# Turning W2 by DMA behind tiles 4 to 11, loading W1 later, and making the blocks of W1 W2^T beside value tiles 16 to 23

## The reference

```
xn  = (x - mean) / sqrt(var + 1e-5)
Q, K, V = xn W1 + b1,  xn W2 + b2,  xn W3 + b3
attn = softmax(Q K^T / 32)
out  = x + (attn V) W4 + b4 + ffn(xn)
ffn: [xr, xi] = split(xn);  [xr Wr^T - xi Wi^T + br,  xr Wi^T + xi Wr^T + bi]
Wr, Wi (512 x 512): unfolded from small tensor-train factors
```

## Time and profile before

| | us |
|---|---|
| median of 3 runs | 1287.73 (1287.54 to 1432.36) |
| profiled execution | 1288.47 |
| its span, slowest core (6) | 1286.9 |
| spans of the 8 cores | 1284.8 to 1286.9 |
| TensorE busy | 1265.2 (98%) |
| VectorE busy | 520.5 (40%) |
| ScalarE busy | 327.0 (25%) |
| GpSimd busy | 169.9 (13%) |

### The profile page before, as it was taken

How to read it: one execution, slowest core, us unless ns; L and a number is a source line. 1 busy time by engine, 2 the same in 40 slices (tenths; PEclk the granted TensorE clock), 3 DMA queues, 4 the chain that set the end, 5 groups by cost and what they waited for, 6 DMA issues and landing times.

```text
span 1286.9 us, 16235 instructions; the slowest of 8 cores (1284.8 to 1286.9 us)
## 1 busy us (share of the span) xinstructions
PE 1265.2 (98%) x5959; PEld 585.4 (45%) x6078; DVE 520.5 (40%) x856; ACT 327.0 (25%) x467; POOL 169.9 (13%) x123
## 2 busy tenths in 40 slices
PE   6999999999999999999999999999999999999998
PEld 4554444444444444444444444444444444444443
DVE  4457460544244414442444244434444244414442
ACT  2453333321211232112222311132212212221111
POOL 2232132211011101111111111111111011101110
PEclk9999999999999999999999999999999999999999
DMA  9899671133122322231233132220332022222222
GB/s 134 196 229 224 150 143 42 33 79 79 41 66 66 66 58 74 66 66 34 77 71 82 33 66 66 66 66 35 79 78 71 34 66 66 66 65 66 66 66 66
DMA packets 187294, 102.83 MB, mean 80 GB/s; under 512 B 169272, under 2 KB 171344, under 8 KB 187216
## 3 DMA queue, kind: packets, MB, share of 16 engines
q1 hardware_dynamic: 181600, 93.37, 31.0%
q0 software_dynamic: 5408, 8.39, 4.5%
q10 hardware_dynamic: 208, 0.02, 0.0%
HBM read 51.43 MB, written 16.78 MB: 53 GB/s over the span
## 4 chain that ended last, share of the span: by engine, by line
PE 98%; DMA 1%; issue 1%; POOL 0%; ACT 0%; DVE 0%; POOLq 0%; ACTq 0%; DVEq 0%
PE ring L795 34%; PE po L837 33%; PE ring L672 9%; PE po L654 4%; PE pf L654 4%; PE pf L822 2%; PE ring L755 2%; PE pf L815 2%; PE pf L808 2%; PE po L709 1%; PE pf L709 1%; DMA V<-W 1%; PE ring L643 1%; PE po L868 1%; PE pf L868 1%
## 5 line engine op out<-in xcount | busy, mean ns | idle before, releaser
L795 PE MATMUL ring<-XT,GT 128*128 128x512 bf16 x2006 | 445.0, 379 | 2.4 <-ACT Et L616 0.2
L837 PE MATMUL po<-V,ET 128*128 128x512 bf16 x1947 | 436.2, 379 | 1.9
L795 PEld LDWEIGHTS ring<-XT,GT 128*128 128x128 bf16 x2048 | 200.3, 98 | 242.1 <-issue 0.6
L837 PEld LDWEIGHTS po<-V,ET 128*128 128x128 bf16 x1984 | 194.1, 98 | 234.1
L482 DVE TENSOR_REDUCE mx<-ring 128x1 f32<-128x512 f32 x256 | 176.7, 690 | 222.0 <-PE ring L795 222.0
L508 DVE SCALAR_TENSOR_TENSOR xr<-po,rrv,xr 128x1024 f32<-128x1024 f32 x31 | 39.8, 1284 | 419.7 <-PE po L837 419.7
L333 POOL TENSOR_TENSOR xr<-xr,cb 128x1024 f32<-128x1024 f32 x32 | 75.1, 2346 | 941.8 <-DVE junk L487 941.8
L611 ACT ACTIVATE S<-ring 128x512 f32<-128x512 f32 x128 | 76.4, 597 | 423.7 <-DVE mx L482 423.6
L616 ACT ACTIVATE Et<-ring,ngm 128x2048 bf16<-128x2048 f32 x32 | 62.9, 1967 | 300.9 <-DVE ngm L501 300.9
L672 PE MATMUL ring<-XT,A 128*128 128x512 bf16 x501 | 111.2, 379 | 0.6
L672 PEld LDWEIGHTS ring<-XT,A 128*128 128x128 bf16 x512 | 50.1, 98 | 60.4
(11 more groups left out here) (97 smaller groups left out, 628.8 us busy)
## 6 DMA issues: line engine op xcount, KB each, us to landing
xr<-x SPq DMA_DIRECT2D x40, 512.0 KB, 3.4
out<-xr SPq DMA_DIRECT2D x31, 512.0 KB, 2.7
S<-x SPq DMA_DIRECT2D x16, 512.0 KB, 5.2
Et<-x SPq DMA_DIRECT2D x8, 512.0 KB, 6.6
V<-W POOLq DMA_DIRECT2D x2, 1024.0 KB, 17.0
V<-W POOLq DMA_DIRECT2D x8, 256.0 KB, 18.2
V<-W POOLq DMA_DIRECT2D x4, 512.0 KB, 20.8
A<-W POOLq DMA_DIRECT2D x4, 512.0 KB, 10.6
```

Of the source, the lines that this page charges most:

```text
L795: mm = e.matmul(bank[tb % 4], GT[:, c, rows(i % 4)], XT[:, c, tb * 512:(tb + 1) * 512], start=(c == 0), stop=(c == 7))
L837: mm = e.matmul(po[:, v * 512:(v + 1) * 512], ET[:, i % 2, tj, :], V[:, tj, v * 512:(v + 1) * 512], start=(tj == 16), stop=(tj == 15))
```

## The change

W2 is no longer turned on TensorE. SP turns its eight units by DMA, one behind the turn and the load of each of the tiles 4 to 11, once the 18 pieces of W3 W4 are made (W2T takes the place of W3T). W1 is loaded behind normalizations 6, 8, 10 and 12 instead of 4 to 7, and turned in steps 16 to 19 instead of 11, 13, 15 and 17; it now waits for all of W2's turns, over whose source it writes. The blocks of W1 W2^T are made in steps 16 to 23 instead of 13 to 20, the small products c behind value tile 12 instead of 9, and the row ub behind value tile 23 instead of 20. VectorE copies c in step 13 instead of 10, and ub in step 24 instead of 21, where it also makes the first addition to cb.

```
-AFOLD = 13
+AFOLD = 16
...
     def step_groups(k):
-        w2 = [("w2", k - 1)] if 1 <= k < 9 else []
-        return ([("xn", k + 2)] if k + 2 < NPE else []) + w2
+        return [("xn", k + 2)] if k + 2 < NPE else []
...  (sync_program)
-            if k in (11, 13, 15, 17):
-
-                p = (k - 11) // 2
+            if 4 <= k < 12:
+
+                m = k - 4
+                if m == 0:
+                    e.wait_ge(s_w34m, 18)
+                e.wait_ge(d_w2[m // 2], 16)
+                e.dma_start_transpose(W2T[:, :, rows(m)], W2raw[:, m, :]).then_inc(d_w2t, 16)
+            elif 16 <= k < 20:
+
+                p = k - 16
                 if p == 0:
-                    e.wait_ge(s_w2tp, 8)
+                    e.wait_ge(d_w2t, 128)
                 e.wait_ge(d_w1[p], 16)
                 for m in (2 * p, 2 * p + 1):
                     e.dma_start_transpose(W1T[:, :, rows(m)], W1raw[:, m, :]
...  (gpsimd_program)
-            elif k in (4, 5, 6, 7):
-                if k == 4:
+            elif k in (6, 8, 10, 12):
+                if k == 6:
                     e.wait_ge(s_gtp, 4)
-                n = k - 4
+                n = k // 2 - 3
                 load_pair(W1raw, w1_d, n, d_w1[n])
...  (vector_program)
-            if k == 10:
+            if k == 13:
                 e.wait_ge(s_cm, 1)
...  (tensor_program)
-            if k == 9:
+            if k == 12:
+                e.wait_ge(d_w2t, 128)
                 small_c()
             elif k == AFOLD + 7:
                 u_row()
```

More of the change, by code:

```diff
@@ L148, in build_nc @@
     s_gtp, s_w3tp, s_w34m = sem("gtp"), sem("w3tp"), sem("w34m")
-    s_xtp, s_vmm, s_w2tp = sem("xtp"), sem("vmm"), sem("w2tp")
+    s_xtp, s_vmm = sem("xtp"), sem("vmm")
     s_cm, s_am, s_ubm = sem("cm"), sem("am"), sem("ubm")
@@ L173, in build_nc @@
     d_g2, d_bb, d_bc = sem("d_g2"), sem("d_bb"), sem("d_bc")
+    d_w2t = sem("d_w2t")
     d_w1t = [sem(f"d_w1t{k}") for k in range(4)]
@@ L355, in evict_group @@
                 return
-            e.wait_ge({"w3": s_w3tp, "xn": s_xtp, "w2": s_w2tp}[kind], n + 1)
-            dst = {"w3": W3T, "xn": XT, "w2": W2T}[kind]
+            e.wait_ge({"w3": s_w3tp, "xn": s_xtp}[kind], n + 1)
+            dst = {"w3": W3T, "xn": XT}[kind]
             e.tensor_copy(dst[:, :, rows(n)], pt[0]).then_inc(s_pt[0], 1)
@@ L635, in turn @@
             else:
[L636 to L639, removed]
+                e.wait_ge(d_w3[n], 16)
+                src, done = W3raw[:, n, :], s_w3tp
             if q >= 2:
```

## The result

The changed kernel takes 1302.58 us (median of four; 1299.15 to 1303.91 in three of them), the kernel before 1288.29. The ratio is 1.0104, interval 1.0090 to 1.0117, so the change costs 13.4 us. (One run of each, 1336.21 and 1432.36 us, had a lowered clock on a whole die; these are in the medians but not in the ratio.) By the bound of 2% this is no change; by its own interval it is a loss. Forecast were 1295 us and no change, in a range of 1284 to 1303.

The account below looks back on a forecast made before the run. TensorE, busy 98%, was taken as the bound, with a nearly full DMA hidden behind it before the attention loop. -3.6 + 10.7 = +7.1 us on 1287.7 gave 1294.8, or 1295 us; range 1284 to 1303.

Parts of the forecast that it names:

- The removed work: Steps 1 to 8: eight turns of W2 leave TensorE, all on the path, saving 3.56 us.
- The mechanism and its place: TensorE idles at value tiles 9 to 12 for turned tiles, 8 to 13 us together, largest at tile 12; attention loop unchanged.
- the lateness of tile 12: Before the attention loop: turned tile 12 lands after TensorE is ready for it, taken as 10.7 us.
- my upper case: At tile 12: W1's fourth pair shares the DMA fully with its turn, adding 4.1 us, so it is late by 12.7.
- Rival B: Tiles 9 to 12: waits also lower TensorE's clock, about 5 us a fall, 1300 to 1305 us; chance 0.13.
- the count of work ahead of tile 12: DMA work queued ahead of turned tile 12, at quiet prices times 1.12: 41.4 us, 46.4 under contention; tested on the old kernel.
- Rival A: Before the attention loop: the DMA keeps up, so all of the 3.6 us is seen, 1284 us; chance 0.22.
- Rival C: Stage end: tile 24's turn and VectorE's step 24 run late, 1.2 + 2 + 2 us more, 1300 us; chance 0.05 (C or more).
- VectorE's step 24: Stage end: ub copies, their sum and the first cb addition ahead of tile 28's shift; 0, at most 2 us.
- the gated tile 24: Stage end: SP can turn tile 24 only once all blocks are made; 0 to 1.2 us.
- VectorE's slower steps 10 to 16: Steps with two weight operations take 4.40 us each while tiles 13 to 15 take 3.45; 0, at most 2 us.
- SP's new wait: Step 4: SP's wait for the 18 products of W3 W4 is met before it is reached; 0.

Follow-up runs that it names:

- experiment 11: Changed kernel with eight unread filler matmuls ahead of TensorE's wait at each of value tiles 8 to 12: 1302.71 us, ratio 1.0114 to the kernel before.
- experiment 1: Changed kernel with only W2's turns put back on TensorE: 1292.69 us, ratio 1.0040 to the kernel before.
- experiment 2: Changed kernel with W2's eight DMA turns left out and made nowhere else: 1291.43 us, ratio 1.0028 to the kernel before.
- experiment 8: Changed kernel with W1 loaded behind normalizations 4, 13, 15, 17 and turned in steps 14, 17, 19, 21: 1293.97 us, ratio 1.0042 to the kernel before.
- experiment 5: Changed kernel with W2 turned on TensorE and W1 loaded behind normalizations 9 to 12: ratio 1.0114 to the kernel before.
- Experiments 1 and 4: Changed kernel with W2 turned on TensorE, 1292.69 us, 1.0040; the same with W1 also loaded behind normalizations 4 to 7, 1289.42 us, 1.0010.
- experiment 3: Changed kernel with W1 loaded behind normalizations 4 to 7 again, W2 still by DMA: 1301.30 us, ratio 1.0096 to the kernel before.
- experiments 5 and 6: Changed kernel with W2 on TensorE and W1 loaded behind normalizations 9 to 12, 1.0114; changed kernel with W1 loaded behind 12 to 15, 1303.43 us, 1.0118.

## Why the prediction was right, and where it was not

**The removed work** (-3.56): right. Without a wait tile 8 would have started at 82.02 + 3.45 = 85.47 on core 3, which is 89.80 less 3.56 and the 0.76 of the earlier start.

**The mechanism and its place**: right for the whole change. TensorE waits for turned tiles, in four pieces and 0.3 us at the first block, the attention loop is unchanged, and the 64 transposes are gone. Tile 12 was forecast to land at 108.7 to 112.8; by the release of normalization 14 it did at 105.8 to 114.8 on the eight cores. Wrong in place: the largest piece on the slowest core is at tile 8, not 12, and it is 6.5 us where I had pieces of 2 to 4.

**The sum** was 6 us short, +7.1 forecast and +13.4 by the runs, and the time lies at the upper edge of the range. The term that was too small is the lateness of tile 12, taken as 10.7 us. On core 3 TensorE would have been ready for it at 85.47 + 4 x 3.45 = 99.27 and began it at 114.56: 15.3 us late, more than the 12.7 of my upper case. With tile 12's 1.67 us at half clock and the 0.33 at the first block, less 3.56 and 0.76, that is the +13.0 again.

**Rival B** (the waits also cost the clock) had 0.13. Its sign came: all eight cores had windows under 1.00 between 80 and 120 us, and the time lies within its 1300 to 1305. But its price of 5 us a fall is not what the slowest core shows. Of the 4.4 us at half clock, the 2.71 of tile 8 are followed by waits for the DMA at tiles 10, 11 and 12, and normalizations 10 to 15 were each released by the DMA and not by TensorE; at full clock these waits would have been longer by as much. Only the 1.67 of tile 12 are left in the chain. This is worked out from one trace; experiment 11 doesn't contradict it and doesn't prove it. The Trainium skill, "TensorE: Matmul & The Clock Gate" (HAM oscillation — how this bites in real kernels), says that DMA waits between groups of matmuls put the clock back. Here the trace agrees for the waits of 6.34 and 2.90 us ahead of tiles 8 and 12, while after 1.25 and 1.42 us on this core the clock stayed up. The length of the wait alone doesn't tell, though: on core 1 of the same execution tile 11 kept full speed (3.61 us) after a wait of 3.20 us, while in experiment 1 (core 7) tile 12 took 5.30 us after 1.96 us.

**The price of a turn.** By the 261 GB/s of the Trainium skill, "DMA: Bandwidth & Descriptors" (Latency and other measured facts), I had estimated tile 12 to be 5 us late. With 15.3 us on core 3 that was further off than the 10.7 from the trace's own rows.

**The cause** was put too narrowly, and experiment 1 shows the step that failed: the count of work ahead of tile 12, with the DMA always busy, told that with W2 on TensorE nothing is lost (tile 12 at 96). It landed at 106. The old kernel passed the test of that count because its loads kept the DMA full from 60 us on the earlier trace rows. The parts, one on top of the other: blocks and small products later, 1.0010; loads behind 6 to 12, 1.0040; W2 by DMA, 1.0104. In us: about +1.3, +3.9 and +8.2, the last after the 3.6 of TensorE, so 9.8 by experiment 2 or 11.8 by this row for the eight DMA turns. The forecast had given all of it to the third part. In these terms the eight turns alone cost about what was forecast for everything (9.8 to 11.8 against 10.7), and the 5.2 us of the other two parts, which I had at nothing, are most of what the sum lacked. That the time still came into the range is in part luck: the range reached to 1303 to take in a fall of the clock, not this. These shares hold for this order of steps only: spreading W1 out, with all of W2 still on the DMA, takes 1.0104 to 1.0042 (experiment 8), and loads behind 9 to 12 lose 1.0114 with nothing of W2 on it (experiment 5). As far as these runs show, the loss comes from turns (of tiles or of W2) and loads meeting, not from the number of turns alone.

**Rival A** (the DMA keeps up) fell, and my argument for it, that the loads are spread over seven normalizations, was one against: spreading moved them from a place with room to beside the turns. **Rival C**: VectorE's step 24 and the gated tile 24 cost nothing on the slowest core here, as forecast. Experiments 1 and 4 show waits of 1.2 to 2.7 us at tile 28 on single cores, within C's sum of 5.2 but over the 2 us that I had as the most for VectorE's step 24. VectorE's slower steps 10 to 16 and SP's new wait cost nothing, as forecast.

What stays open: why some cores get a stretch of 10 us at 91 to 158 GB/s and others don't, in the same execution; whether the pairs do harm because they convert from f32, or by their amount alone, as no run has a load of the same size without conversion; and the net price of the half clock.

## What to carry to other kernels

A hidden resource that is full is a bound in waiting: before moving work onto it, count what must pass it ahead of each deadline, and check in which windows it is really busy, for work put off out of an idle window is paid a second time beside the urgent work. Small savings on the bounding engine (here 3.6 us) are lost to a single late transfer. In the trace worked through here, a half-clock stretch cost time only where no later wait swallowed it: count the lateness of the last late tile, not the sum of all that was slow. Undo each part of a change alone: the part named in the forecast was about six tenths of the loss.

## What the hardware showed beyond the forecast

- The issue of a DMA turn of 128x1024 holds SP for 1.2 us when unhindered. Where the DMA share stood over 1 it held SP for up to 8.3 us in the changed kernel (core 1) and 13.5 us in experiment 3 (core 5); everything after it in SP's program is then late too.
- With a converting load (f32 to bf16) in flight beside them, turns of normalized tiles took 8.9 us (experiment 1, tile 12), 12.9 from issue to landing (changed kernel, core 3) and at most 15.4 and 15.1 us (experiments 5 and 6), against at most 9.2 in the kernel before on any core. Stretches of 5 to 10 us show a DMA share of 1.0 to 1.3 at 91 to 121 GB/s. Part of that low figure is bookkeeping, as a pair counts with the 0.52 MB of bf16 that it writes (8.39 MB for 16 pairs) and not with the f32 that it reads; the late turns are not.
- The slowest core decides, and it is another one from run to run: spans within one execution were 2.1 us apart before and 7.7 us after.
